# Spreading the router's logits over four steps of TensorE, and moving one weight subtraction from VectorE to GpSimd

## The chip, the cores and the metric

The kernel runs on one core of one Trainium2 chip. The metric is the device time of one execution in microseconds, lower is better. The engines are named as in the profile: PE is TensorE (PEld its weight loads), DVE is VectorE, ACT is ScalarE, POOL is GpSimd, and SP is the queue that issues most of the DMAs.

## The reference, cut to what matters

Eight sequences of 512 tokens with 256 features go through four residual layers: attention, a mixture of eight SwiGLU experts with the best two taken, a Mamba block, and a second mixture of eight experts. Every layer is fed the layer norm of x.

```python
x = L0_attn_x                                   # (8, 512, 256)
x = x + _L0_attn_ref(_layernorm(x), ...)        # 16 heads of 16, rotary, softmax, out projection
x = x + _L0_ffn_ref(_layernorm(x), ...)         # 8 experts, top 2, F = 352
x = x + _L1_attn_ref(_layernorm(x), ...)        # Mamba block, inner 512, state 16
x = x + _L1_ffn_ref(_layernorm(x), ...)         # 8 experts, top 2

# the router of the first expert layer, of which the change moves a part
logits = x @ router_weight                      # (4096, 256) @ (256, 8)
probs = softmax(logits, axis=-1)
_, topk_idx = top_k(probs, 2)
```

## The kernel before, in words

The four layers are phases, one behind the other. The change touches only the first, `attention_phase`, in which the attention runs, and beside it the routing of the tokens for the first expert layer, and the preparation of the first experts' weights.

The phase is a software pipeline written out by hand. The outer loop `for t in SLOTS` has a slot for each of 32 tiles (one is four heads of one sequence, `t` = 0 to 31) and some ahead and behind. In a slot TensorE has 16 steps, `for k in range(16)`. In each step it does one matmul of transposed scores for tile t (`scores_T`, line 983, into one of two banks `t_ps`) and one of plain scores for tile t + 2 (`scores`, line 992, into `s_ps`). ScalarE takes the exponent of each transposed score (`exp`, line 550). VectorE takes row maxima of the plain scores, eight in a slot, one for two steps (`max_pair`, line 706). TensorE may run two steps ahead of `exp`, and its `scores` of maximum m waits for `max_pair` m - 2; the last maximum of a slot is number 8u + 8. Steps 2, 6, 10 and 14 have the product with the values besides (`values`, line 1003), step 3 the transpose of the maxima (line 1009), step 8 the query and key product for a later sequence (`queries_keys`, line 1019), step 12 the value projection.

The routing goes sequence by sequence (`batch(t, lag)` says which, every fourth slot). Four slots carry it on: lag 10 transposes normalised rows, lag 11 makes the logits, lag 12 and 13 choose the experts and count places. The logits of one sequence are four token tiles (`logits(n, a, bank)`, a = 0 to 3, line 1059), with two products each in full fp32, eight columns wide, into the one bank `f_ps`, which is shared with steps 8 and 12, with the transpose of the maxima and others. `take_bank` keeps them apart: it waits for whatever must have emptied the bank, and its argument is what the next user has to wait for. `r_z` says that VectorE has taken the logits out (`differences`, lines 774 and 775, between the third and the fourth `max_pair` of its slot); they wait for `r_logits`, which comes with token tile a = 3. The lag 11 slots in this loop are t = 11, 15, 19, 23 and 27. The logits of the last three sequences are made in slots 30 and 31 and behind, with code of their own.

The weights of expert k of the next layer are loaded while attention still runs, and split into an upper part in fp32r and a remainder: ScalarE makes the upper part (`upper_piece`, line 115), another engine subtracts (`lower_parts`, line 129, two operations of 128x1088). For expert 0 ScalarE does it in slot 27, and VectorE subtracts in its tail, between `take_rows(n - 1, 1, ...)` and `differences(n - 1, ...)`, while TensorE is in slot 30. Expert 1 follows later in the same tail. The next phase's TensorE waits for `lo_done` ahead of its first tile.

POOL in a slot: Newton steps for a normalisation (`newton`, lines 282 to 288, if there is a sequence for it, as in slot 29), the split of the maxima (lines 481 and 483), the split of queries and keys, `merge_heads` (lines 458, 460, 463), then layer norm, the bias (line 429) and the scatter of rows (line 443). Its loop for slot 28 ends with `merge_heads(27)`.

## Time and profile before

| | |
|---|---|
| median of 3 runs | 2119.03 us (2118.62 to 2119.91) |
| the profiled execution | 2119.03 us |
| its span, first to last instruction | 2117.2 us |
| mean granted TensorE clock | 0.943 of full |
| busy | PE 1884.2, DVE 1654.2, ACT 1280.1, POOL 1427.7 us |

Busy shares are means over phases with different limits, so they say little about one phase. What lies around the span is the difference of 1.8 us to the execution's own time. The granted clock is given as a share of full speed: 1.00 is 2.4 GHz and 0.50 is 1.2 GHz. Line numbers are those of the kernel before.

### The profile page before, as it was taken

The numbers are of one execution on the slowest core, as the hardware profiler recorded it, in microseconds if no ns is written. First come the engines' busy times: TensorE is split into PE (matmuls) and PEld (weight loads), VectorE is DVE, ScalarE is ACT, GpSimd is POOL, SyncE is SP. The second block draws the span as 40 slices with busy tenths as digits, with TensorE's granted clock in tenths as the row PEclk, the third lists the DMA queues.
The fourth block names the chain that finished last, engine by engine and source line by source line (L and its number), as shares of the span: only waits on it lengthen the run. The fifth ranks groups of instructions, "written<-read, shape, count | busy, mean of one in ns | idle before, by whom it ended". The sixth has DMA issues, their size and how long they took to land.

```text
span 2117.2 us, 32322 instructions
## 1 busy us (share of the span) xinstructions
PE 1884.2 (89%) x9878; PEld 1104.5 (52%) x9878; DVE 1654.2 (78%) x2242; ACT 1280.1 (60%) x2736; POOL 1427.7 (67%) x1238
## 2 busy tenths in 40 slices
PE   3699999999974999966899999999999999779998
PEld 2344444444444999963445454535353544247776
DVE  4588888888855656530899999999999999976664
ACT  3177766677753433326787878777777766734443
POOL 4344545543352444430999999999999999966665
PEclk8599999999976999987999999999999999999999
DMA  5766665555254544640313030405040405200100
GB/s 106 120 103 115 104 104 117 121 122 117 61 178 127 105 74 77 139 104 28 152 50 131 33 148 10 171 1 179 0 180 0 171 0 182 89 30 29 37 27 29
DMA packets 231395, 194.35 MB, mean 92 GB/s; under 512 B 147219, under 2 KB 200235, under 8 KB 230716
## 3 DMA queue, kind: packets, MB, share of 16 engines
q1 hardware_dynamic: 205498, 163.33, 29.1%
q0 software_dynamic: 13296, 17.77, 5.0%
q10 hardware_dynamic: 12434, 11.18, 1.9%
q8 instruction: 85, 1.39, 0.3%
q14 instruction: 82, 0.67, 0.1%
HBM read 138.15 MB, written 54.08 MB: 91 GB/s over the span
## 4 chain that ended last, share of the span: by engine, by line
POOL 34%; PE 12%; issue 7%; ACT 1%; DVE 1%; DMA 0%; POOLq 0%; DVEq 0%; ACTq 0%
POOL mb_dbu L2191 22%; POOL mb_hp L2197 10%; PE mb_da_ps L2003 9%; POOL mb_dtu L2203 1%; PE mb_f_ps L2433 1%; PE mb_f_ps L1964 1%; PE mb_f_ps L2437 0%; PE mb_f_ps L2451 0%; PE mb_y_ps L1982 0%; PE mb_f_ps L1953 0%; PE mb_f_ps L2441 0%; DVE mb_da_ps L2373 0%; DVE mb_hp L2371 0%; ACT mb_res L2267 0%; ACT mb_xin L2270 0%
## 5 line engine op out<-in xcount | busy, mean ns | idle before, releaser
L2191 POOL TENSOR_TENSOR mb_dbu<-mb_dtu,mb_bbc 128x1024 f32<-128x1024 f32 x256 | 599.2, 2366 | 5.2 <-DVE mb_da_ps L2373 2.4
L550 ACT ACTIVATE ex_plain<-at_t_ps 128x512 f32<-128x512 f32 x512 | 289.7, 596 | 170.8 <-PE at_t_ps L983 169.6
L2373 DVE TENSOR_TENSOR_SCAN mb_da_ps<-mb_da_ps,mb_dbu 128x1024 f32<-128x1024 f32 x160 | 365.3, 2283 | 4.6 <-ACT mb_da_ps L2245 3.3
L2414 PE MATMUL mb_y_ps<-mb_hc,lw_ident 128*128 128x512 f32 x640 | 314.6, 615 | 38.6 <-DVE mb_hc L2380 37.9
L706 DVE TENSOR_REDUCE at_mx<-at_s_ps 128x2 f32<-128x1024 f32 x256 | 310.7, 1218 | 33.2 <-PE at_s_ps L992 31.2
L992 PE MATMUL at_s_ps<-ex_w 48*128 48x512 f32 x512 | 226.1, 499 | 16.1 <-DVE at_mx L706 16.1
L983 PE MATMUL at_t_ps<-ex_w 64*128 64x512 f32 x512 | 219.8, 483 | 12.2 <-ACT ex_plain L550 6.9
L2197 POOL TENSOR_TENSOR mb_hp<-mb_hp,mb_cbc 128x1024 f32<-128x1024 f32 x96 | 226.7, 2361 | 0.0
L2371 DVE TENSOR_TENSOR_SCAN mb_hp<-mb_da_ps,mb_dbu 128x1024 f32<-128x1024 f32 x96 | 218.9, 2280 | 8.5 <-POOL mb_dbu L2191 7.4
L1390 POOL DMA_INDIRECT x<-m_o,m_xs x71 | 113.7, 1601 | 163.3 <-DMA x<-m_o,m_xs 85.1
L2414 PEld LDWEIGHTS mb_y_ps<-mb_hc,lw_ident 128*128 128x128 f32 x640 | 118.9, 193 | 198.3 <-issue 127.7
L2380 DVE TENSOR_TENSOR mb_hc<-mb_da_ps,mb_cbc 128x1024 f32<-128x1024 f32 x160 | 195.4, 1221 | 12.5
L2414 PE MATMUL mb_y_ps<-mb_hp,lw_ident 128*128 128x512 f32 x384 | 185.5, 606 | 14.5 <-POOL mb_hp L2197 14.5
L983 PEld LDWEIGHTS at_t_ps<-ex_w 64*128 64x128 f32 x512 | 85.7, 191 | 177.4 <-ACT ex_plain L550 148.0
L2244 ACT ACTIVATE mb_da_ps<-mb_dt,lw_a_neg 128x512 f32<-128x512 f32 x256 | 172.6, 674 | 0.0
L2245 ACT ACTIVATE mb_da_ps<-mb_dt,lw_a_neg 128x511 f32<-128x511 f32 x256 | 171.9, 671 | 0.0
L2243 ACT ACTIVATE mb_da_ps<-mb_zero 128x1 f32<-128x1 f32 x256 | 43.0, 168 | 203.3 <-DVE mb_hc L2380 162.8
L1495 PE MATMUL m_y_ps<-ex_w,m_xsT_hi 128*128 x568 | 157.2, 338 | 0.0
L1003 PE MATMUL at_o_ps<-ex_plain 128*32 128x512 f32 x1024 | 143.6, 634 | 0.8 <-ACT ex_plain L550 0.7
L1645 POOL TENSOR_TENSOR m_odd<-m_odd,m_odd_in 128x256 f32<-128x256 f32 x96 | 70.8, 737 | 94.0 <-ACT m_odd_in L1765 89.4
L2414 PEld LDWEIGHTS mb_y_ps<-mb_hp,lw_ident 128*128 128x128 f32 x384 | 73.9, 195 | 105.2 <-issue 78.0
L1901 DVE SCALAR_TENSOR_TENSOR m_x<-mb_da_ps,m_small,m_x 128x256 f32<-128x256 f32 x128 | 61.8, 483 | 79.5 <-PE mb_da_ps L2003 76.8
(355 smaller groups left out, 4097.9 us busy)
## 6 DMA issues: line engine op xcount, KB each, us to landing
mb_bbc<-mb_scr SPq DMA_DIRECT2D x64, 512.0 KB, 5.9
mb_cbc<-mb_scr SPq DMA_DIRECT2D x64, 512.0 KB, 6.4
ex_w<-at_scr SPq DMA_DIRECT2D x126, 128.0 KB, 3.8
m_xs<-rt_rows SPq DMA_DIRECT2D x71, 129.0 KB, 2.2
at_scr<-at_qk_hi SPq DMA_DIRECT2D x32, 256.0 KB
ex_w<-at_scr SPq DMA_DIRECT2D x126, 64.0 KB, 3.8
at_scr<-at_qk_lo SPq DMA_DIRECT2D x28, 256.0 KB
at_xin<-in_x SPq DMA_DIRECT2D x32, 128.0 KB, 3.9
```

The source lines that it names most:

```text
L550: act.activation(probs[:, c, h, :], t_ps[:, k % 2, :], ACT.Exp, scale=SCALE).then_inc(exp_done, 1)
L706: dve.tensor_reduce(out, s_ps[:, m % 2, :, :], AX.X, ALU.max).then_inc(max_done, 1)
L983: pe.matmul(t_ps[:, k % 2, :], of_head(kst, r, h, 64, c), of_head(qst, r, h, 64), start=True, stop=True).then_inc(t_ready, 1)
L992: last = pe.matmul(s_ps[:, m % 2, a, :], of_head(qst, u % 4, h + 2 * a, 48, c), of_head(kst, u % 4, h + 2 * a, 48), start=True, stop=True)
L2003: last = pe.matmul(L.o_ps[:, u % 4, :], rows, w[:, e, kt, :], start=(m == 0), stop=(m == 5))
L2191: pool.tensor_tensor(dbu[:, q % 3, :, :], dtu_2, bbc[:, 2 * p:2 * p + 2, :], ALU.mult).then_inc(S["dbu_ready"], 1)
L2197: pool.tensor_tensor(hp[:, r, :, :], hp[:, r, :, :], cbc[:, 2 * p:2 * p + 2, :], ALU.mult).then_inc(S["hp_ready"], 1)
L2244: act.activation(da_ps[:, q % 2, 0, :], dt[:, d % 2, :], ACT.Exp, scale=a_neg[:, d, 2 * p:2 * p + 1])
L2371: dve.tensor_tensor_scan(hp[:, t % 3, :, :].rearrange("p j t -> p (j t)"), da, add, 0.0, ALU.mult, ALU.add).then_inc(S["scan_done"], 1)
L2373: dve.tensor_tensor_scan(da, da, add, 0.0, ALU.mult, ALU.add).then_inc(S["scan_done"], 1)
L2380: dve.tensor_tensor(hc[:, t % 2, :, :], da_ps[:, r, :, :], cbc[:, 2 * p:2 * p + 2, :], ALU.mult).then_inc(S["hc_ready"], 1)
L2414: last = pe.matmul(y_ps[:, v % 2, :], ident[:, :], src[:, j, :], start=False, stop=(q == tile_last[v] and j == 1))
```

## The change

Two edits. The logits of a sequence are made one token tile in each of the steps 4, 5, 6 and 7, where there were two in step 4 and two in step 5; the wait for `r_z` is set behind the last of them. And `lower_parts` of expert 0 is called by POOL at the end of its slot 28, no longer by VectorE in its tail.

```diff
@@ attention_phase, gpsimd @@
                     if (n := batch(t, 13 + c)) is not None:
                         pool.wait_ge(v_ps_ready, min(t + 3, NT))
                         scatter(n, c)
+                if t == 28:
+                    experts.lower_parts(pool, 0)
                 if t == NT - 1:
                     scatter(NB - 3, 0)
@@ attention_phase, vector @@
             take_rows(n - 1, 1, score_bank(3))
-            experts.lower_parts(dve, 0)
             differences(n - 1, score_bank(0))
@@ attention_phase, tensor @@
-                    if k in (4, 5) and (n := batch(t, 11)) is not None and t < NT - 2:
-                        f_free = take_bank([(R["r_z"], n + 1)] if k == 5 else [])
-                        logits(n, 2 * (k - 4), f_ps)
-                        logits(n, 2 * (k - 4) + 1, f_ps)
+                    if 4 <= k < 8 and (n := batch(t, 11)) is not None and t < NT - 2:
+                        f_free = take_bank([(R["r_z"], n + 1)] if k == 7 else [])
+                        logits(n, k - 4, f_ps)
```

## Rows read from the trace of the kernel before

**Rows 1.** The page, part 4: the chain that ended last, by engine

```profile
POOL 34%; PE 12%; issue 7%; ACT 1%; DVE 1%; DMA 0%; POOLq 0%; DVEq 0%; ACTq 0%
```

**Rows 2.** Waits, 110 to 600 us: who waited for whom, us, times, longest

```profile
ACT ex_plain L550 <- PE at_t_ps L983: 145.2, 187, 2.1
...
DVE at_mx L706 <- PE at_s_ps L992: 28.9, 61, 2.0
```

**Rows 3.** Slots 8, the five with logits (first, last, sum), and 28

```profile
core 0: us, PE busy (x) PEld busy (x) DVE busy (x) ACT busy (x) POOL busy (x), PEclk, DMA share, GB/s
220.06:235.15 15.09, 14.77 (x143) 6.64 (x142) 13.06 (x20) 10.86 (x24) 8.52 (x20) 1.00 0.67 107
...
266.95:287.97 21.02, 19.96 (x160) 9.68 (x158) 15.22 (x27) 10.84 (x23) 8.21 (x13) 0.84 0.61 112
...
535.32:552.87 17.55, 17.10 (x152) 8.11 (x150) 12.72 (x21) 12.27 (x25) 4.61 (x5) 0.81 0.29 72
sum 94.82, PE 91.67 PEld 45.00 DVE 70.85 ACT 55.26 POOL 41.38; mean PE 18.33 PEld 9.00 DVE 14.17 ACT 11.05 POOL 8.28
...
552.87:567.03 14.16, 13.53 (x136) 5.63 (x134) 13.75 (x24) 11.42 (x24) 5.01 (x11) 1.00 0.26 63
```

**Rows 4.** Stretch ahead of the first fall; first two of five falls; their sum

```profile
266.70:270.10 3.40, 3.21 (x23) 2.27 (x21) 2.85 (x5) 2.33 (x5) 0.72 (x2) 1.00 1.14 282
270.10:276.90 6.80, 6.80 (x22) 3.01 (x22) 2.84 (x8) 2.20 (x4) 0.00 (x0) 0.50 0.43 69
341.80:345.20 3.40, 3.40 (x13) 2.18 (x10) 1.43 (x3) 1.60 (x3) 0.28 (x1) 0.50 0.51 128
...
sum 23.60, PE 23.34 PEld 10.10 DVE 10.64 ACT 10.53 POOL 2.88; mean PE 4.67 PEld 2.02 DVE 2.13 ACT 2.10 POOL 0.57
```

**Rows 5.** Timeline of slot 11, PE and DVE: start, us, engine, line, idle before

```profile
267.84 1.06 PE L1059 MATMUL at_f_ps<-at_rw,at_wraw 128*128 128x8 f32 x8 [0.18 <-ACT at_nm L601]
...
269.26 1.14 PE L1059 MATMUL at_f_ps<-at_rw,at_wraw 128*128 128x8 f32 x8
...
269.39 1.23 DVE L706 TENSOR_REDUCE at_mx<-at_s_ps 128x2 f32<-128x1024 f32 x1 [0.43 <-PE at_s_ps L992]
...
270.54 0.18 DVE L774 TENSOR_REDUCE at_zmax<-at_f_ps 128x4 f32<-128x32 f32 x1
...
273.78 1.23 DVE L706 TENSOR_REDUCE at_mx<-at_s_ps 128x2 f32<-128x1024 f32 x1 [2.03 <-PE at_s_ps L992]
...
277.03 0.75 DVE L866 TENSOR_SCALAR at_qk<-at_f_ps,at_bqk 128x512 f32<-128x512 f32 x1 [2.03 <-PE at_f_ps L1019]
```

**Rows 6.** Timeline of VectorE's tail and TensorE's slot 30

```profile
588.89 3.56 DVE L129 TENSOR_TENSOR ex_w<-ex_plain,ex_w 128x1088 fp32r<-128x1088 f32 x2
...
591.39 1.06 PE L1059 MATMUL at_s_ps<-at_rw,at_wraw 128*128 128x8 f32 x8
...
592.48 0.19 DVE L774 TENSOR_REDUCE at_zmax<-at_s_ps 128x4 f32<-128x32 f32 x1
```

**Rows 7.** Timeline, POOL and DVE side by side; L782 over all (ns min/median/max)

```profile
282.39 2.36 POOL L429 TENSOR_TENSOR ex_plain<-ex_plain 128x1024 f32<-128x1024 f32 x1
...
283.36 1.45 DVE L782 TENSOR_TENSOR at_pr<-at_pr,at_scale 128x32 f32<-128x32 f32 x1
...
623.32 1.53 POOL L463 TENSOR_TENSOR ex_plain<-ex_plain,at_rsum 128x512 f32<-128x512 f32 x1
...
623.55 1.35 DVE L726 TENSOR_TENSOR at_masks<-at_ties,at_rank 128x32 f32<-128x32 f32 x1
...
L782 DVE TENSOR_TENSOR at_pr<-at_pr,at_scale x8: 191/306/1445, 283.4 to 645.9; 128x32 f32<-128x32 f32 x8
```

**Rows 8.** Timeline around the end of slot 28: POOL, DVE and PE

```profile
560.51 1.54 POOL L463 TENSOR_TENSOR ex_plain<-ex_plain,at_rsum 128x512 f32<-128x512 f32 x1
...
563.33 0.19 DVE L720 TENSOR_TENSOR at_ties<-at_left,at_pay 128x32 f32<-128x32 f32 x1
...
563.85 1.23 DVE L706 TENSOR_REDUCE at_mx<-at_s_ps 128x2 f32<-128x1024 f32 x1
...
565.27 0.40 PE L983 MATMUL at_t_ps<-ex_w 64*128 64x512 f32 x1
```

## The prediction, made before the result was known

> **What bounds the kernel now.** I read the page first, its chain that ended last: 34% of the span is POOL, from lines of the Mamba phase [rows 1]. Both edits lie far ahead of that, in the attention phase, roughly the first third of the span. The later phases start when it is done, so what it gains or loses at its own end reaches the end of the kernel in full; the question is what sets its pace. The waits show that no engine does alone: ScalarE waited 145 us for transposed scores of TensorE, and VectorE 29 us for its plain scores [rows 2]. TensorE, VectorE and ScalarE run in a ring, two steps apart, and over a whole slot TensorE and VectorE are both nearly full. Time by slot shows it: slot 8, with no routing product, took 15.09 us with TensorE busy for 14.77 and VectorE for 13.06. The five slots that hold the router's logits (t = 11, 15, 19, 23, 27) took 21.02 us in the first and 17.55 in the last, 94.82 us together, and slot 28 took 14.16 us with VectorE busy for 13.75 of them [rows 3].
>
> Then I asked why the logits slots are so long, by short stretches. Each has a fall of the granted clock to 1.2 GHz, half of 2.4: five falls, 23.6 us together, in which TensorE was busy for 23.34. Ahead of the first it had been busy for 3.21 of 3.40 us at full clock, so that it was not idle before it fell; but it streamed only eight columns per matmul in the logits [rows 4]. The first logits products and those of the next step take 1.06 and 1.14 us, with one pair of score matmuls between them, and the fall begins as they end [rows 5].
>
> **The change part by part.**
> *Logits spread over four steps (k = 4 to 7) in place of two.* The same eight matmuls a slot (16 records), nothing added: about 0.53 us for one token tile (half of 1.06), 2.1 us for four [rows 5]. Spread out, steps 4 to 7 each hold one score pair and 0.53 us of logits, and the attention product of step 6 now stands in the middle of the logits, not behind them. If that keeps the clock up, the gain is at most half of the falls, as the engine was busy all through: 23.6 / 2 = 11.8 us.
> Against it stands VectorE's order. It takes the logits between its third and fourth maximum of the slot (L774 between two L706). The third began at 269.39 in slot 11 and took 1.23 us; logits were ready then, and L774 began at 270.54 with no wait [rows 5]. Worked through at full clock from 267.84: logits end at 268.4, pair of step 5 at 268.8, logits 269.3, pair of step 6, attention product to 270.7, logits 271.2, pair of step 7, last logits 272.2. The third maximum is done at 270.2, so VectorE now waits 2.1 us, with the fourth maximum, ready at 271.7, queued behind. The two small operations are done at 272.75. TensorE is released for the query and key product of step 8 (it uses the same bank) about 0.25 us later than it gets there, and step 10's scores, which need the fourth maximum, about 0.1 us late: 0.35 us a slot for TensorE. VectorE then ends its fourth maximum at 274.8 in place of 275.0 (273.78 + 1.23), takes the query chunk right behind it at 274.8, where it took it at 277.03 [rows 5]. So of the 3.4 us that the fall of 6.8 us cost, 2.2 come back and 1.2 stay with VectorE's new wait. I take the same 1.2 off in each of the five: 11.8 - 6.0 = 5.8 us gained if no fall is left. If all five are left, nothing comes back and TensorE's 0.35 us is paid five times: 1.7 us lost. The rows don't show which it will be: the products are half as thick, but the thin stretch is longer, 4.4 us (267.84 to 272.2) in place of 2.5 (to 270.4), with an attention product in it. I take the middle: (5.8 - 1.7) / 2 = 2.0 us gained.
>
> *The subtraction for expert 0 off VectorE's tail.* Two subtractions of 128x1088 ran there from 588.89 for 3.56 us. Right behind them L774 began at 592.48; but the logits it reads are TensorE's, from 591.39 for 1.06 us, up to 592.45 [rows 6]. What is late next is therefore already there: VectorE would have waited to 592.45 anyhow, and the gain is 0.03 us, taken as nothing. It can't be more unless those logits come sooner, and they are as they were.
>
> *The same subtraction on POOL at the end of slot 28.* It waits for ScalarE's upper pieces of slot 27, long made. POOL's merge of heads ends at 562.05 (560.51 + 1.54); the two operations follow at once. Price: the trace has POOL at 2.36 us for 128x1024, so 2.36 x 1088 / 1024 = 2.51 us each, 5.0 us, up to 567.1 [rows 7, 8]. Queued behind on POOL are the seven small Newton steps, whose result ScalarE wants in step 4 of slot 29, and the split of the maxima, whose rows TensorE wants a slot later; both would be late by a microsecond or two at most, and ScalarE stands in that time anyway, by what follows.
> What is not hidden is VectorE. Where POOL reads SBUF in a tensor operation, a VectorE operation with two SBUF inputs stands still: L782, a 128x32 product begun at 283.36, took 1.45 us and ended at 284.81, with POOL's 128x1024 addition from 282.39 to 284.75; its shortest is 0.19. Two in a row are each held by a POOL operation of their own: L726, at 623.55, stood to 624.90 for the POOL operation that began at 623.32, before it [rows 7]. In slot 28 VectorE begins such an operation at 563.33 (L720), the next one behind it, and then the last maximum at 563.85 [rows 8]. The first is held to POOL's end at 564.6; POOL's second operation then takes its turn and holds L721 to 567.1. The last maximum begins at 567.2: 3.4 us late. TensorE needs it for its scores in step 2 of slot 29, to which it came at 565.27, and stands for 3.2 us, ScalarE behind it. VectorE has next to no slack to make it good (0.4 us in slot 28 [rows 3]). So +3.4 us; the bounds are 0 (POOL elsewhere when these two come) and 3.4.
> The Trainium skill, SBUF — State Buffer, "Who interferes with whom", has the pair of ports shared as an exclusive lock for the whole instruction, for two-input VectorE operations against GpSimd reads, and no conflict for a reduction. By this rule the sum is the same 3.4; were the hold only a sharing of bandwidth, it would be about 0.4 us. The row, which ends with POOL's operation, agrees.
> The stand of 3.2 us may also bring a fall of TensorE's clock in slot 29. The falls after the logits were 3.4 or 6.8 us; one of 3.4 costs 0 (VectorE sets the pace) to 1.7 us. I take 0.5.
>
> Sum: -2.0 + 0 + 3.4 + 0.5 = +1.9 us on the profiled execution's own 2119.03, which is also the median of the three runs: 2120.9 us.
>
> **The rivals.**
> *All falls go, and POOL's hold is paid.* -5.8 + 3.4 + 0.5 = -1.9: 2117.1 us. For it: each fall follows the two thick clumps of logits. Against it: the thin stretch gets longer.
> *Falls go and the hold misses.* If VectorE reaches its two small operations in slot 28 before 562, or after 567, there is no hold: -2.0 to -5.8, about 2114.5 us. It speaks for it that slot 27's falls end differently and may shift the two engines against each other; against it, that 5 us of POOL must miss a pair of operations in a slot where VectorE never idles.
> *Slower: the falls stay and the hold is paid with a fall behind it.* +1.7 + 3.4 + 1.7 = +6.8: 2125.8 us. Its place is the last maximum of slot 28, and it decides once at most one of the five falls goes (from +0.2% = 4.2 us on).
> The Trainium skill, TensorE: Matmul & The Clock Gate, "Why this matters for your kernels", puts drops down to idle gaps between bursts. By it the spread would leave the clock as it is and the hold in slot 28 would bring a fall, which is the slower case. The rows disagree in part, as the clock fell after stretches in which the engine was busy throughout.
>
> **How the numbers follow.** A difference of 0.2%, 4.2 us, is about what a measurement here can tell from none. Chances: the likeliest case (hold paid, about half of the falls gone, 2117.5 to 2123.2) 0.48; all falls gone with the hold 0.14; hold missed 0.14, of which 0.10 reaches beyond 0.2%; slower 0.24. So faster 0.12 (the 0.10 and a tail of the second case), same 0.65, slower 0.23. The range goes from the sum of the best bounds (-5.8 with a little over the hold's zero, 2114) to near the worst (2126).
>
> **What would show it.** In the changed kernel: L1059 in groups of four records, one a step; a wait of about 2 us of VectorE for L1059 ahead of L774 in the five slots; the granted clock in those slots, five falls or fewer; on POOL two operations of L129 of 2.5 us near 560; L720 and L721 behind them at over 1 us each, then a wait of TensorE's L992 for L706 of about 3 us, and slot 28 to 29 longer than 14.16 us by as much; L774 in the tail waiting for L1059 at about its old distance. The prediction is wrong if the five slots shorten by over 8 us, if L721 stays at 0.19 us, or if the tail's L774 moves forward by more than the rest.

## The result, and the profile after

The changed kernel is slower: a median of 2136.55 us (2134.21 to 2138.44, 4 runs) against 2119.47 us of the kernel before in the same series (2118.62 to 2122.36, 4 runs). The ratio is 1.0078, with a 95% interval of 1.006 to 1.0095, or 17.1 us by the medians. The forecast was 2120.9 us within 2114 to 2126: no change was the likeliest case, and the time lies outside the range on the side of the slower rival, beyond it too. The profiled execution took 2136.86 us, its span is 2135.1 us, and the mean granted clock 0.939. One operation of `lower_parts` stands on line 129 in both kernels; most lines of the attention phase are one or two further on (L706 is now L708, L720 and L721 are L722 and L723, L774 is L776, L983 is L984, L992 is L993, L1003 is L1004, L1059 is L1060).

The page's chain that ended last is word for word the line of [rows 1]: the later phases are as they were, and what the attention phase loses reaches the end.

The waits of 110 to 600 us (who waited for whom, us, times, longest). Against [rows 2] ScalarE waits 9 us more for transposed scores, and VectorE has a wait for the logits that is new:

```profile
ACT ex_plain L552 <- PE at_t_ps L984: 153.8, 186, 3.7
...
DVE at_zmax L776 <- PE at_f_ps L1060: 16.6, 5, 4.1
```

Time by slot, from one transpose of the maxima to the next, as in [rows 3]: slot 8, then the logits slots 11, 15, 19, 23 and 27, then 28 and 29.

```profile
218.98:234.07 15.09, 14.78 (x144) 6.65 (x142) 13.08 (x20) 10.87 (x24) 8.52 (x20) 1.00 0.66 102
265.87:288.35 22.48, 21.62 (x159) 10.66 (x158) 15.20 (x27) 11.06 (x23) 8.26 (x13) 0.77 0.58 110
337.56:360.04 22.48, 21.63 (x159) 10.67 (x157) 15.26 (x27) 11.06 (x23) 11.63 (x18) 0.77 0.59 132
409.15:430.68 21.53, 21.34 (x160) 10.67 (x158) 13.85 (x25) 10.79 (x21) 9.29 (x11) 0.76 0.49 114
479.61:496.84 17.23, 16.87 (x157) 8.60 (x155) 13.69 (x23) 10.89 (x21) 7.68 (x8) 1.00 0.64 146
540.84:558.73 17.89, 16.51 (x151) 7.77 (x150) 12.59 (x21) 12.49 (x25) 4.58 (x5) 0.90 0.30 68
558.73:576.04 17.31, 14.05 (x136) 5.72 (x134) 16.97 (x25) 11.43 (x24) 9.90 (x13) 1.00 0.24 52
576.04:594.98 18.94, 18.41 (x136) 7.77 (x134) 12.09 (x22) 12.46 (x24) 6.16 (x8) 0.64 0.07 24
```

Slot 8 is the same to 0.01 us. The five logits slots take 101.61 us in place of 94.82. Their share of half clock can be read from the column PEclk: at 0.77 a slot of 22.48 us has 2 x 0.23 x 22.48, about 10.3 us, at 1.2 GHz. Slots 11, 15 and 19 have a fall of 10.2 us each, slot 23 has none and is the one that got shorter, and slot 27 has one of 3.4. That last one is of another kind: it begins 8.0 us into the slot, behind 3.4 us in which TensorE was busy for only 2.20. Slot 28 goes from 14.16 to 17.31 us at full clock, so by a stand and not by the clock, and slot 29 from 14.46 to 18.94 us at 0.64.

That makes an account of the 17.8 us by which the two spans differ: -1.1 before slot 11 starts, +6.8 in the five logits slots, +0.15 in the slots between, +3.15 in slot 28, +4.5 in slot 29, and +4.3 from slot 30 to the end. The last of these goes with the clock too. These are the 110 us from the start of slot 30, before and after:

```profile
581.49:691.49 110.00, 68.86 (x318) 46.67 (x318) 61.84 (x170) 49.16 (x94) 45.17 (x46) 0.67 0.47 148
594.98:704.98 110.00, 69.96 (x302) 45.07 (x302) 55.53 (x163) 46.84 (x89) 42.06 (x44) 0.63 0.47 148
```

By the same reading that is about 73 us at 1.2 GHz before and 81 after. The first matmul of line 1495, in the next phase, starts 89.2 us after slot 30 before and 91.9 after, so that 2.7 of the 4.3 us are already there.

The first fall of 10.2 us in three pieces, with the 3.4 us ahead of it, to be read against [rows 4]:

```profile
265.50:268.90 3.40, 3.21 (x23) 1.97 (x25) 3.29 (x6) 2.42 (x6) 0.72 (x2) 1.00 1.10 279
268.90:272.30 3.40, 3.40 (x15) 1.41 (x8) 0.20 (x1) 0.60 (x2) 0.00 (x0) 0.50 0.91 136
272.30:275.70 3.40, 3.40 (x11) 2.55 (x12) 2.31 (x7) 1.62 (x3) 0.00 (x0) 0.50 0.02 7
275.70:279.10 3.40, 3.40 (x15) 0.98 (x13) 1.98 (x2) 1.64 (x4) 1.46 (x2) 0.50 0.02 5
```

TensorE was busy for 3.21 of 3.40 us ahead of it, as in the kernel before, and for all of each of the three pieces. The timeline of the same slot, PE and DVE, against [rows 5]:

```profile
266.77 0.61 PE L1060 MATMUL at_f_ps<-at_rw,at_wraw 128*128 128x8 f32 x4 [0.19 <-ACT at_nm L603]
...
267.73 0.61 PE L1060 MATMUL at_f_ps<-at_rw,at_wraw 128*128 128x8 f32 x4
...
268.70 1.79 PE L1004 MATMUL at_o_ps<-ex_plain 128*32 128x512 f32 x8
270.43 1.02 PE L1060 MATMUL at_f_ps<-at_rw,at_wraw 128*128 128x8 f32 x4
...
272.10 1.02 PE L1060 MATMUL at_f_ps<-at_rw,at_wraw 128*128 128x8 f32 x4
...
273.16 0.19 DVE L776 TENSOR_REDUCE at_zmax<-at_f_ps 128x4 f32<-128x32 f32 x1 [4.06 <-PE at_f_ps L1060]
```

The clock falls after the second group. The attention product and the last two groups run at half speed, 1.79 us for what takes 1.06 and 1.02 us for 0.61, and VectorE stands for 4.06 us where it stood for none.

The end of slot 28, POOL, DVE and PE, against [rows 8]:

```profile
567.87 4.95 POOL L129 TENSOR_TENSOR ex_w<-ex_plain,ex_w 128x1088 fp32r<-128x1088 f32 x2
...
569.20 1.23 DVE L722 TENSOR_TENSOR at_ties<-at_left,at_pay 128x32 f32<-128x32 f32 x1
...
570.47 2.40 DVE L723 TENSOR_TENSOR at_ties<-at_ties,at_order 128x32 f32<-128x32 f32 x1
...
572.90 1.23 DVE L708 TENSOR_REDUCE at_mx<-at_s_ps 128x2 f32<-128x1024 f32 x1
...
574.18 0.50 PE L993 MATMUL at_s_ps<-ex_w 48*128 48x512 f32 x1 [2.63 <-DVE at_mx L708]
```

This went as forecast, operation by operation: two subtractions of 4.95 us together, each of which holds one of VectorE's two operations to its own end (1.23 and 2.40 us in place of 0.19 each), the last maximum right behind, and TensorE's stand for it.

The tail, against [rows 6]:

```profile
604.87 1.06 PE L1060 MATMUL at_s_ps<-at_rw,at_wraw 128*128 128x8 f32 x8
605.96 0.19 DVE L776 TENSOR_REDUCE at_zmax<-at_s_ps 128x4 f32<-128x32 f32 x1 [3.50 <-PE at_s_ps L1060]
```

The subtraction of 3.56 us is gone and a wait of 3.50 us stands there. L776 comes 10.98 us after the start of slot 30 (594.98), before it was 10.99 (592.48 from 581.49).

### The profile page after: what moved, and what is told of

The parts are those of the page before. It is cut to its first block, busy times and chain, and to the rows that moved or that the text cites. A ratio compares the mean times of both kernels' runs of the same rounds, so it can differ in the third digit from the quotient of the medians.

```text
span 2135.1 us, 32322 instructions
## 1 busy us (share of the span) xinstructions
PE 1896.7 (89%) x9878; PEld 1108.9 (52%) x9878; DVE 1653.4 (77%) x2240; ACT 1282.4 (60%) x2736; POOL 1431.0 (67%) x1240
## 4 chain that ended last, share of the span: by engine, by line
POOL 34%; PE 12%; issue 7%; ACT 1%; DVE 1%; DMA 0%; POOLq 0%; DVEq 0%; ACTq 0%
POOL mb_dbu L2191 22%; POOL mb_hp L2197 10%; PE mb_da_ps L2003 9%; POOL mb_dtu L2203 1%; PE mb_f_ps L2433 1%; PE mb_f_ps L1964 1%; PE mb_f_ps L2451 0%; PE mb_y_ps L1982 0%; PE mb_f_ps L2437 0%; PE mb_f_ps L1953 0%; PE mb_f_ps L2441 0%; DVE mb_da_ps L2373 0%; DVE mb_hp L2371 0%; ACT mb_res L2267 0%; ACT mb_xin L2270 0%
## 5 line engine op out<-in xcount | busy, mean ns | idle before, releaser
L708 DVE TENSOR_REDUCE at_mx<-at_s_ps 128x2 f32<-128x1024 f32 x256 | 310.7, 1218 | 30.4 <-PE at_s_ps L993 28.5
L993 PE MATMUL at_s_ps<-ex_w 48*128 48x512 f32 x512 | 228.8, 504 | 19.0 <-DVE at_mx L708 17.4
L984 PE MATMUL at_t_ps<-ex_w 64*128 64x512 f32 x512 | 224.1, 493 | 11.0 <-ACT ex_plain L552 5.8
L984 PEld LDWEIGHTS at_t_ps<-ex_w 64*128 64x128 f32 x512 | 87.5, 195 | 175.3 <-ACT ex_plain L552 141.9
L1004 PE MATMUL at_o_ps<-ex_plain 128*32 128x512 f32 x1024 | 148.7, 655 | 0.8 <-ACT ex_plain L552 0.7
```

Of the source, the lines that this page charges most:

```text
L708: dve.tensor_reduce(out, s_ps[:, m % 2, :, :], AX.X, ALU.max).then_inc(max_done, 1)
L984: pe.matmul(t_ps[:, k % 2, :], of_head(kst, r, h, 64, c), of_head(qst, r, h, 64), start=True, stop=True).then_inc(t_ready, 1)
L993: last = pe.matmul(s_ps[:, m % 2, a, :], of_head(qst, u % 4, h + 2 * a, 48, c), of_head(kst, u % 4, h + 2 * a, 48), start=True, stop=True)
```

## The experiments

All were timed beside the kernel before, in three series, in which its median was 2120.75 us (2113.54 to 2125.43, 27 runs), 2119.95 us (2113.03 to 2126.1, 35 runs) and 2118.75 us (2113.38 to 2125.4, 23 runs). The first two series ran on one chip. The third ran on another: the whole change with the hold taken out, half of the hold, the changed kernel once more, and the two pairs far apart. The ratios are the ones to go by: single executions of one kernel differ by up to 13 us here. A fall that is given a length below was read off the granted clock of that run's trace.

### The parts of the change

**The spread alone.**

```diff
-                    if k in (4, 5) and (n := batch(t, 11)) is not None and t < NT - 2:
-                        f_free = take_bank([(R["r_z"], n + 1)] if k == 5 else [])
-                        logits(n, 2 * (k - 4), f_ps)
-                        logits(n, 2 * (k - 4) + 1, f_ps)
+                    if 4 <= k < 8 and (n := batch(t, 11)) is not None and t < NT - 2:
+                        f_free = take_bank([(R["r_z"], n + 1)] if k == 7 else [])
+                        logits(n, k - 4, f_ps)
```

> The logits are spread over steps 4 to 7, and the subtraction stays in VectorE's tail. Theory 1 (the spread itself lengthens the clock falls: three falls of 10.2 us in slots 11, 15 and 19 of the changed kernel, where they were 6.8, 3.4 and 3.4): the start of slot 28 comes 6.9 us later than before, as in the changed kernel, and the total is about 2126 us, 7 above before. Rival 2 (the spread costs nothing lasting, the whole 17 us comes from POOL's operations): 2119 plus or minus 1 us. Rival 3 (the spread gains by itself, as I worked it out, and only together with the other edit is it lost): 2113 to 2117 us.

Measured: 2129.46 us median (2113.54 to 2132.45, 11 runs), ratio 1.0032 (1.0014 to 1.0051), or about 6.8 us slower. Its slots 11, 15 and 19, and the sum of the five:

```profile
268.29:286.94 18.65, 17.53 (x159) 8.90 (x158) 15.18 (x27) 11.12 (x23) 8.22 (x13) 1.00 0.69 127
336.15:358.56 22.41, 21.55 (x159) 10.77 (x157) 15.25 (x27) 11.05 (x23) 11.68 (x18) 0.77 0.58 130
407.64:429.44 21.80, 21.58 (x160) 10.71 (x158) 14.21 (x25) 10.77 (x21) 9.30 (x11) 0.77 0.51 115
...
sum 99.32, PE 95.40 PEld 47.72 DVE 70.92 ACT 56.31 POOL 41.45; mean PE 19.08 PEld 9.54 DVE 14.18 ACT 11.26 POOL 8.29
```

The same instructions give two kinds of slot. Slot 11 has no fall and takes 18.65 us, 2.4 less than before; slots 15 and 19 have one of 10.2 us each and take 2.9 and 3.3 more. So the spread is a gamble: its fastest run, 2113.54 us, equals the fastest of the kernel before in that series, and in most executions it loses. Slot 28 starts at 558.78 us, 5.9 later than before, as in the changed kernel (558.73); the 6.9 of the expectation was a slip.

**The second edit alone.**

```diff
+                if t == 28:
+                    experts.lower_parts(pool, 0)
...
-            experts.lower_parts(dve, 0)
```

> POOL does the subtraction of expert 0 at the end of slot 28; the logits stay two and two. Theory 1 (VectorE's two-input operations are held to the end of POOL's, TensorE then stands for about 3 us, and a clock fall follows it): slot 28 is 3.2 us longer, slot 29 some 4 us, L721 takes over 2 us, total about 2129 us, 10 above before. Rival 2 (the hold alone, no fall): 2122.5 us. Rival 3 (it costs nothing without the spread, since VectorE and POOL meet differently): 2119 us.

Measured: 2126.44 us (2124.44 to 2134.03, 10 runs), ratio 1.0037 (1.0023 to 1.005). Its slots 28 and 29:

```profile
552.24:569.74 17.50, 14.22 (x136) 5.71 (x134) 17.12 (x26) 11.45 (x24) 9.93 (x13) 0.99 0.23 52
569.74:586.36 16.62, 15.62 (x135) 6.43 (x133) 11.94 (x21) 12.36 (x24) 5.95 (x8) 0.81 0.08 27
```

Slot 28 has 3.3 us more by the hold, and slot 29, in which nothing was changed, 2.2 more with a fall of 6.8 us behind TensorE's stand (some 4 were expected).

**The subtraction on GpSimd in slot 30.** The same work off VectorE, but not where it holds anything.

```diff
+                if t == NT - 2:
+                    experts.lower_parts(pool, 0)
                 if (u := tile(t - 1)) is not None:
                     merge_heads(u)
...
-            experts.lower_parts(dve, 0)
```

> As the last one, but POOL does the same two operations in slot 30, ahead of its merge of heads 29, where VectorE has no operation with two SBUF inputs. If the price of slot 28 is the hold of VectorE and not POOL's own time: same as before, 2118 to 2120 us, no VectorE operation longer than before, and L774 in the tail still waits for TensorE's logits (gain of taking the subtraction off VectorE: nothing). Rival (any 5 us of POOL late in attention delays the chain, or the subtraction in VectorE's tail was on the path): 2122 us or more, or below 2116 us.

Measured: 2119.12 us (2113.88 to 2125.59, 11 runs), ratio 0.9996 (0.9981 to 1.0012). In the timeline GpSimd works from 584.77, and VectorE's tail waits as in the changed kernel:

```profile
584.77 4.95 POOL L129 TENSOR_TENSOR ex_w<-ex_plain,ex_w 128x1088 fp32r<-128x1088 f32 x2
...
594.08 0.19 DVE L776 TENSOR_REDUCE at_zmax<-at_s_ps 128x4 f32<-128x32 f32 x1 [3.50 <-PE at_s_ps L1060]
```

So 5 us of GpSimd's time cost nothing there, and 3.56 us less of VectorE's tail gain nothing.

**The whole change with the hold taken out:** the spread, and the subtraction in slot 30, both as above.

> The whole change, but GpSimd subtracts in its slot 30 and not at the end of slot 28, where VectorE begins two operations with two SBUF inputs. Theory 1 (the second edit costs only by its place): as the spread alone, 2125 to 2130 us, with slot 28 at 14.2 us, L721 at 0.19 us and no fall behind it in slot 29. Rival (the two edits hurt each other through the shared bank and the tail): 2133 us or more.

Measured: 2126.66 us (2116.61 to 2130.97, 12 runs), ratio 1.0033 (1.0019 to 1.0048), the ratio of the spread alone. Slots 28 and 29 took 14.18 and 14.45 us at full clock. With this and the last run, the second edit costs by its place alone.

**Half of the hold.** Of the two subtractions the first on GpSimd in slot 28, the second in VectorE's tail, behind a wait for the first.

```diff
+    def lower_half(self, eng, k, i):
+        eng.wait_ge(self.hi_done, k + 1)
+        if i:
+            eng.wait_ge(self.half_done, 1)
+        hi, lo, raw = self.piece(k, i, 2)
+        eng.tensor_tensor(lo, raw, hi, ALU.subtract).then_inc(self.lo_done if i else self.half_done, 1)
...
+                if t == 28:
+                    experts.lower_half(pool, 0, 0)
...
-            experts.lower_parts(dve, 0)
+            experts.lower_half(dve, 0, 1)
```

> The second edit alone and half of it: the first of the two subtractions on GpSimd at the end of slot 28, the second stays in VectorE's tail. Two of them in slot 28 gave 5.7 us more, 3.3 of it in slot 28 and 2.1 in slot 29 by a fall of 6.8 us behind TensorE's stand. Theory 1 (each GpSimd subtraction holds one of VectorE's two operations to its own end): L720 held to about 564.7, L721 at 0.19 us, the last maximum some 0.9 us late, no fall in slot 29: 2120 to 2122.5 us. Rival (the cost is not by the hold but by GpSimd's lateness for its Newton steps and the split of the maxima): half of 5.7, about 2123 to 2124 us, with L721 short in both.

Measured: 2119.98 us (2115.96 to 2122.83, 12 runs), ratio 1.0001 (0.999 to 1.0012). The timeline (here L730 and L731 are the two operations), and slots 28 and 29:

```profile
559.42 2.51 POOL L130 TENSOR_TENSOR ex_w<-ex_plain,ex_w 128x1088 fp32r<-128x1088 f32 x1
...
560.76 1.23 DVE L730 TENSOR_TENSOR at_ties<-at_left,at_pay 128x32 f32<-128x32 f32 x1
562.02 0.19 DVE L731 TENSOR_TENSOR at_ties<-at_ties,at_order 128x32 f32<-128x32 f32 x1
```

```profile
550.27:565.38 15.11, 14.07 (x136) 5.74 (x134) 14.77 (x25) 11.44 (x24) 7.53 (x12) 1.00 0.25 59
565.38:579.82 14.44, 13.22 (x135) 5.53 (x133) 11.86 (x22) 12.14 (x24) 5.95 (x8) 1.00 0.09 31
```

One subtraction holds one operation. Slot 28 is 0.95 us longer, and behind this shorter stand the clock does not fall. The price is not in proportion: one subtraction costs 0.95 us, two cost 3.3 in slot 28 and a fall as well. The rival was that GpSimd's lateness for its Newton steps costs the time. They began 11.75 us after the start of slot 28 here, where they began 10.19 before and 14.17 in the changed kernel. So this run rules out that 1.6 us of lateness cost anything: slot 29 took 14.44 us. For the 4.0 us of the changed kernel its own trace answers: in its slot 29 ScalarE's waits are all for TensorE, none for GpSimd.

**The changed kernel once more,** word for word.

> The changed kernel once more, word for word, for a second profile of it beside the others. Its two parts alone gave 2129.5 (spread) and 2126.4 us (subtraction on GpSimd in slot 28) against 2120.75, 8.7 and 5.7 us. Theory 1: the parts add up, 2133 to 2137 us, and the logits slots show falls of 10.2 us or none at all, never of 3.4 us; slot 28 is 17.3 us long again. Rival: the first profile was a poor draw, and the kernel is nearer to 2128 us.

Measured: 2137.91 us (2129.56 to 2142.56, 5 runs), ratio 1.0081 (1.006 to 1.0103). Its profile is of the fastest of these executions, and shows slots 11, 15 and 19, the sum of the five, and slots 28 and 29 thus:

```profile
268.03:289.44 21.41, 20.36 (x159) 10.50 (x157) 15.20 (x27) 10.96 (x23) 8.23 (x13) 0.84 0.61 113
338.66:357.31 18.65, 17.53 (x160) 8.89 (x158) 15.24 (x27) 11.11 (x23) 11.64 (x18) 1.00 0.72 154
406.39:423.96 17.57, 17.20 (x159) 8.86 (x158) 13.74 (x25) 10.89 (x21) 9.31 (x11) 1.00 0.58 132
...
sum 93.99, PE 89.70 PEld 45.72 DVE 70.46 ACT 56.31 POOL 41.46; mean PE 17.94 PEld 9.14 DVE 14.09 ACT 11.26 POOL 8.29
...
553.16:571.96 18.80, 15.53 (x135) 5.96 (x133) 17.37 (x26) 11.44 (x24) 9.95 (x13) 0.91 0.21 48
571.96:590.83 18.87, 18.34 (x135) 7.77 (x134) 11.86 (x20) 12.48 (x24) 6.16 (x8) 0.64 0.07 24
```

The same kernel, other falls: slots 15 and 19 have none and take 3.8 and 4.0 us less than in its first profile. My theory that a spread slot has a fall of 10.2 us or none was too neat: slots 11 and 27 have one of 6.8 each. Slots 28 and 29 are the other way: 9.0 us more than in the kernel before, with one fall of 17.1 us that begins in slot 28, which took 18.80 us and not 17.3.

### What the falls come from

**One token tile a slot.** In the five slots only token tile 3 is computed; the logits of tiles 0 to 2 of those sequences are left out.

```diff
-                    if k in (4, 5) and (n := batch(t, 11)) is not None and t < NT - 2:
-                        f_free = take_bank([(R["r_z"], n + 1)] if k == 5 else [])
-                        logits(n, 2 * (k - 4), f_ps)
-                        logits(n, 2 * (k - 4) + 1, f_ps)
+                    if k == 5 and (n := batch(t, 11)) is not None and t < NT - 2:
+                        f_free = take_bank([(R["r_z"], n + 1)])
+                        logits(n, 3, f_ps)
```

> Leaves work out: in the slots 11, 15, 19, 23 and 27 only the logits of token tile 3 are made (step 5), so that the router of the first five sequences reads what else lies in the bank. It prices the logits and their falls together. Theory 1 (the falls come from TensorE's thin products): hardly a fall is left in the five slots, each 15.5 to 16.5 us, 94.8 us down to about 80, total about 2105 us. Rival (the falls come from something else in those slots, such as the wait for the maxima in step 3): five falls stay, and the total is at most 8 us (5 x 1.6) below before, 2111 us.

Measured: 2104.33 us (2101.27 to 2106.62, 4 runs), ratio 0.9925 (0.9904 to 0.9946). The five slots:

```profile
266.70:283.17 16.47, 15.57 (x148) 7.08 (x146) 15.01 (x27) 10.67 (x23) 8.22 (x13) 1.00 0.74 132
...
sum 77.39, PE 74.78 PEld 34.02 DVE 69.67 ACT 54.43 POOL 41.48; mean PE 14.96 PEld 6.80 DVE 13.93 ACT 10.89 POOL 8.30
```

None has a fall, and they take 17.4 us less. The products that were left out are worth 5 x 3 x 0.53 = 8.0 us at full clock, so more than half of it is the clock (and VectorE's waits). In these slots it is the thin products that bring the falls. They are not the only thing that does: slot 26, which has no logits, has a fall of 3.4 us in this run and in the kernel before. There TensorE was less busy ahead of it; before:

```profile
522.40:525.80 3.40, 2.42 (x14) 1.01 (x16) 3.31 (x7) 2.77 (x6) 0.00 (x0) 1.00 0.25 45
```

**The spread with VectorE's take moved.** Of the possible reasons for the long falls, VectorE's new wait was the one to take away first. The logits are spread as in the change, the subtraction stays in the tail, and VectorE takes the logits behind its fourth maximum.

```diff
-                if (n := batch(t, 11)) is not None:
-                    differences(n, f_ps)
...
                 max_pair(ahead, 3)
+                if (n := batch(t, 11)) is not None:
+                    differences(n, f_ps)
```

> Logits spread over steps 4 to 7 as in the change, with nothing on GpSimd, and VectorE takes them behind its fourth maximum and no longer ahead of it. The spread alone gave 2129.5 us, with clock falls of 10.2 us in two of the five logits slots of its profile and none in two others. Theory 1: the falls are so long because the thin products now lie over four steps; VectorE's order is not their cause: falls of 0 or 10.2 us again, 2127 to 2131 us. Theory 2: VectorE's wait for the last logits, with the fourth maximum queued behind it, starves TensorE at half clock and keeps the fall alive: without that wait the falls are 3.4 or 6.8 us as in the kernel before, 2117 to 2122 us. In both TensorE may stand some 0.5 us a slot ahead of the query and key product of step 8, since its bank now comes free behind the fourth maximum.

Measured: 2125.81 us (2113.62 to 2130.66, 12 runs), ratio 1.0023 (1.0007 to 1.0039). VectorE doesn't wait for logits any more in slot 11, and the five slots sum to about what they did:

```profile
277.37 0.18 DVE L774 TENSOR_REDUCE at_zmax<-at_f_ps 128x4 f32<-128x32 f32 x1
```

```profile
269.70:292.17 22.47, 21.63 (x159) 10.71 (x158) 15.20 (x27) 11.06 (x23) 8.27 (x13) 0.77 0.59 108
...
sum 100.21, PE 96.50 PEld 48.05 DVE 71.01 ACT 56.04 POOL 41.26; mean PE 19.30 PEld 9.61 DVE 14.20 ACT 11.21 POOL 8.25
```

Falls of 10.2 us in slots 11, 15 and 19 again, so the wait is not their cause. The median is lower than that of the spread alone and 1.2 us below the range of the first theory, but the two intervals overlap: whether the moved take gains a little is open.

**All four token tiles in step 5.** The other way round: thicker and shorter.

```diff
-                    if k in (4, 5) and (n := batch(t, 11)) is not None and t < NT - 2:
-                        f_free = take_bank([(R["r_z"], n + 1)] if k == 5 else [])
-                        logits(n, 2 * (k - 4), f_ps)
-                        logits(n, 2 * (k - 4) + 1, f_ps)
+                    if k == 5 and (n := batch(t, 11)) is not None and t < NT - 2:
+                        f_free = take_bank([(R["r_z"], n + 1)])
+                        for a in range(4):
+                            logits(n, a, f_ps)
```

> All four token tiles of logits in step 5, eight matmuls (16 records) in one stretch of 2.1 us, no others moved. Theory 1 (what counts is over how long a stretch the thin products lie): the falls get shorter or rarer than in the kernel before, 0 or 3.4 us in place of 3.4 and 6.8: 2110 to 2117 us. Rival (what counts is how thick they lie): falls of 6.8 us or more in all five slots, 2122 us or above. Either way TensorE's bank and VectorE's take of the logits stand as in the kernel before.

Measured: 2116.84 us (2114.47 to 2120.11, 12 runs), ratio 0.999 (0.9977 to 1.0002). The falls are of 3.4 us in slots 11, 15 and 19 and of 6.8 in 23 and 27; the five slots sum to 93.73 us. The time fits the first theory (2110 to 2117), the ratio can't tell it from no change, and all five falls are there, as the rival had it. Thick and short is at any rate better than thin and long.

**Two groups with the query and key product between them.** One token tile in each of the steps 4, 5, 9 and 10. VectorE takes two tiles where it took four, and the other two behind its fifth maximum (the lines that call it there are left out below); `r_half` and `r_zh` are new semaphores for the first half.

```diff
+            def half_differences(n, h):
+                z_in = f_ps[:, 2 * h * E0:(2 * h + 2) * E0].rearrange("p (k e) -> p k e", k=2)
+                dve.wait_ge(R["r_logits"] if h else R["r_half"], n + 1)
+                steps(dve.tensor_reduce(zmax[:, 2 * h:2 * h + 2], z_in, AX.X, ALU.max))
+                zb = zmax[:, 2 * h:2 * h + 2].unsqueeze(2).broadcast_to([P, 2, E0])
+                dve.tensor_tensor(pr[:, 2 * h:2 * h + 2, :], z_in, zb, ALU.subtract).then_inc(R["r_z"] if h else R["r_zh"], 1)
...
-                    if k in (4, 5) and (n := batch(t, 11)) is not None and t < NT - 2:
...
+                    if k in (4, 5, 9, 10) and (n := batch(t, 11)) is not None and t < NT - 2:
+                        a = (4, 5, 9, 10).index(k)
+                        f_free = take_bank([(R["r_zh"], n + 1)] if a == 1 else [(R["r_z"], n + 1)] if a == 3 else [])
+                        logits(n, a, f_ps)
```

> The four token tiles in two groups with the query and key product between them: one tile each in steps 4, 5, 9 and 10, VectorE takes the first two where it took all four, and the other two behind its fifth maximum; ScalarE's exponent of the logits goes from step 10 to step 11. Theory 1 (falls come where thin products lie close together, and not otherwise; with a single tile a slot there was no fall and the five slots took 77.4 us together): no falls, 77.4 + 5 x 3 x 0.53 = 85.4 us for the five slots in place of 94.8, so 9.4 less on 2120.75: about 2111 us. Rival (the number of thin products in a slot decides, wherever they stand): falls as before or as in the spread, 2120 to 2130 us. A wait of some 0.5 us of TensorE ahead of step 9's logits, for VectorE's take of the query chunk, may come on top, five times: 2 us.

Measured: 2114.72 us (2111.82 to 2118.82, 12 runs), ratio 0.9978 (0.9968 to 0.9987). The five slots sum to 89.29 us, with falls of 3.4 us in slots 11 and 15 and none in the others: neither theory in full, and faster than the kernel before by its interval.

**The second group in step 10 alone.** As the last one, but tiles 2 and 3 back to back in step 10.

```diff
+                    if k in (4, 5) and (n := batch(t, 11)) is not None and t < NT - 2:
+                        f_free = take_bank([(R["r_zh"], n + 1)] if k == 5 else [])
+                        logits(n, k - 4, f_ps)
+                    if k == 10 and (n := batch(t, 11)) is not None and t < NT - 2:
+                        f_free = take_bank([(R["r_z"], n + 1)])
+                        logits(n, 2, f_ps)
+                        logits(n, 3, f_ps)
```

> As the split version, but the last two token tiles stand together in step 10, behind the product with the values, where the bank is long free. Theory 1: no falls, about 2111 us, without the wait in step 9. If two tiles back to back (1.06 us) are enough for a fall by themselves, one is seen that begins in step 10 or 11, and the time is between this and 2120.75 us. Rival (the number of thin products in a slot decides): 2120 to 2130 us.

Measured: 2116.37 us (2113.3 to 2122.34, 12 runs), ratio 0.9988 (0.9978 to 0.9999). The five slots sum to 88.31 us, with falls of 3.4 us in slots 11, 15 and 19. They begin 2.5 to 2.8 us into the slot, so ahead of step 10: it is the first group that brings them, and the second, back to back, brings none.

**Two pairs, far apart.** Tiles 0 and 1 back to back in step 5, tiles 2 and 3 in step 10 as in the last one.

```diff
+                    if k == 5 and (n := batch(t, 11)) is not None and t < NT - 2:
+                        f_free = take_bank([(R["r_zh"], n + 1)])
+                        logits(n, 0, f_ps)
+                        logits(n, 1, f_ps)
```

> The logits in two pairs, two token tiles back to back in step 5 and two in step 10, with the query and key product between them. One tile each in steps 4, 5, 9 and 10 gave 2114.7 us, two falls of 3.4 in four slots; steps 4, 5 and a pair in 10 gave 2116.4 us with three; all four in step 5 2116.8 us with three of 3.4 and two of 6.8. Theory 1 (closeness counts, two pairs far apart are short enough): at most two falls of 3.4 us, 2112 to 2116 us. Rival (a pair is as bad as four): 2117 us or more, with falls in all five slots.

Measured: 2112.2 us (2109.09 to 2114.13, 6 runs), ratio 0.9957 (0.9942 to 0.9972): the fastest that does the whole work, by 9 us against the kernel before. Slot 23, and the sum of the five:

```profile
469.28:484.98 15.70, 15.65 (x157) 8.16 (x155) 13.60 (x24) 10.57 (x21) 7.62 (x8) 1.00 0.66 146
...
sum 87.19, PE 84.99 PEld 42.02 DVE 72.11 ACT 54.92 POOL 41.43; mean PE 17.00 PEld 8.40 DVE 14.42 ACT 10.98 POOL 8.29
```

Three falls of 3.4 us, in slots 11, 15 and 19, where at most two were expected, and none in 23 and 27. Its interval lies below that of the version with steps 4, 5 and a pair in 10, and just overlaps that of the single tiles; both of those were timed in another series, on the other chip.

How many falls one profile shows doesn't tell these versions apart. The run with half of the hold, in which the logits stand as before, has none in slots 23 and 27 either. It allows a comparison without the clock, though. Its slot 23:

```profile
472.66:489.35 16.69, 16.39 (x158) 8.23 (x156) 13.81 (x23) 10.65 (x21) 7.68 (x8) 1.00 0.63 148
```

With the two pairs the slot takes 15.70 us, also at full clock: 1.0 us less with the same products. Slot 27 took 15.06 against 15.47, both without a fall, and slots 15 and 19 took 19.10 and 18.25 against 19.51 and 18.53 in the kernel before, with a fall of 3.4 us in each of the four. So by these profiles some 2 us of the 9 are the order of the work and not the clock.

## Why the prediction was wrong

Point by point, by its own steps.

*The spread: this is the step that failed.* The prediction said "I take the middle: (5.8 - 1.7) / 2 = 2.0 us gained". It measured 6.8 us lost (3 to 11 by the interval). The mistake is in the bounds under it: "If all five are left, nothing comes back" let a fall that stays be as long as it was, 3.4 or 6.8 us, so that the worst was TensorE's 0.35 us five times. The falls that stayed were mostly longer: 10.2 us in two to three of the five slots in four of the five profiles with spread logits. Over the five slots together these profiles have 34.0, 27.2, 30.6, 37.4 and 13.6 us at half clock, and the four in which the logits stand as before 23.8, 27.2, 27.2 and 13.6. The slots themselves sum to 94.0 to 102.7 us, mean 99.6, against 91.4 to 96.6, mean 94.8. So two single profiles could have shown it either way, and it is the ratios that show the loss. The text named the reason, a thin stretch of 4.4 us in place of 2.5, and used it only against the gain, never for a loss. The 0.35 us itself held: with a fall of 6.8 us in both, slot 11 took 21.41 us spread (the changed kernel's second profile) and 21.02 before, 0.39 more. The upper bound was right in kind: where no fall came, slots 15 and 19 took 18.65 and 17.57 us against 19.51 and 18.53 of before, though these had only 3.4 us at half clock each. Put together from the slots without a fall of the different spread profiles (18.65, 18.65, 17.57, 17.23 and 15.59 us), the five would take 87.7 us, 7.1 less than before, where 5.8 were forecast. The half of its length that a fall was taken to cost at most has a clean pair now, slot 15 of the changed kernel: 22.48 us with a fall of 10.2 and 18.65 with none, 3.8 us where half would be 5.1.

*VectorE's new wait.* Forecast as 2.1 us at full clock in each of the five slots, and 2.23 us in slot 23, the one without a fall. In the five together it was 16.6 us, 3.3 on average, and 4.06 in slot 11, where the fall began between the groups. It was there, and it was not the cause of the falls, as the version with the take moved shows.

*The subtraction off the tail.* Forecast as nothing, and nothing it was: 10.98 us into slot 30 in place of 10.99, and a ratio of 0.9996 where it was done alone in a harmless place.

*GpSimd's hold in slot 28.* Forecast 3.4 us; measured 3.15 in the changed kernel and 3.3 in the second edit alone. The order (first operation to the end of the first subtraction, second to the end of the second) was right, and TensorE's stand was near, 2.63 us where 3.2 were forecast. The Trainium skill, SBUF — State Buffer, "Who interferes with whom", has this as an exclusive lock for the whole instruction, and the traces agree: 1.23 and 2.40 us for operations of 0.19, each ending with GpSimd's. The rows show besides that two VectorE operations in a row are held by two of GpSimd's in a row, one each.

*The fall behind the stand.* Taken as 0.5 us, at most 1.7, from falls of 3.4 us. This term was mis-sized: the falls were 6.8, 13.6 and 17.1 us long in the three profiles with both subtractions in slot 28, and slot 29 took 2.2, 4.5 and 4.4 us more (with 1.3 more in slot 28 in the last). A stretch of the trace shows how idle TensorE was ahead of the fall: busy for 1.92 of 3.40 us in the changed kernel, where it was busy for all of them at this place before. The first line is of the kernel before, the other two of the changed one.

```profile
563.69:567.09 3.40, 3.40 (x23) 1.47 (x19) 3.19 (x7) 2.17 (x4) 0.99 (x5) 1.00 0.00 0
572.70:576.10 3.40, 1.92 (x12) 0.59 (x12) 3.30 (x7) 0.00 (x0) 1.58 (x8) 1.00 0.00 0
576.10:589.70 13.60, 13.16 (x107) 5.97 (x107) 8.54 (x17) 8.65 (x17) 2.20 (x4) 0.50 0.01 4
```

In the other two profiles it was busy for 1.60 and 0.90 of the 3.40 us. The trace of the kernel before had a warning that the bound left out, since it was taken from the logits slots alone: from 601.20 to 631.90 us, in the tail, TensorE ran at half clock for 30.7 us in one piece, busy for 23.06 of them.

The Trainium skill, TensorE: Matmul & The Clock Gate, "Why this matters for your kernels", puts drops in the middle of a kernel down to idle gaps between bursts of matmuls; the fall in slot 29 is of that kind, though its stand, 2.63 us, is a little shorter than the gap that the row names. Those in the five logits slots of the kernel before are not, as TensorE was busy for 3.21 to 3.40 of the 3.40 us ahead of each, and the version with one token tile a slot has none. There the measurement decides.

*The sum.* 6.8 us for the spread and 7.8 for the second edit (0.37% of 2120.75) make 14.6, and the whole change measured 0.78% and 0.81%, 16.5 to 17.2. Within the intervals the parts add up. The slower rival had the right mechanisms (hold and fall behind it, nothing gained by the spread) and stopped at 2125.8 us because it let no fall be longer than those in the logits slots of the one profile of before. The rival with the hold missed has a slip in its sum that changed nothing: -2.0 to -5.8 on 2119.03 is 2113.2 to 2117.0, so its middle is 2115.1, and its lower end lies below the range's 2114.

*What stays open.* Why a fall over spread logits mostly lasts 10.2 us and one over dense ones 3.4 or 6.8 was not isolated. What is shown is the order of the times over the spacings, and that VectorE's order is not the reason. Nor is it known what sets the length of the fall behind the stand: 1.60, 1.92 and 0.90 of 3.40 us busy were followed by 6.8, 13.6 and 17.1. The 4.3 us from slot 30 on look like a draw of the clock and not an effect: the same kernel took 1536.9 us for that stretch in its second profile, with a mean clock of 0.67 over the 110 us from slot 30 as in the kernel before, and the twelve experiments took 1534.9 to 1540.2.

## What to carry to other kernels

Where a bound is taken from the length of the falls in one profile, it is not a bound: a change that makes a thin stretch longer, or adds a stand, can make a fall longer than those that the profile shows in that place, so that the worst case needs a term of its own. In this kernel small matmuls that stream few columns were better kept in short groups with dense work between the groups (ratio 0.9957) than thinned out over four neighbouring steps (1.0032); that is worth trying elsewhere, and part of the gain was not the clock's. And work that is moved to GpSimd costs nothing or several microseconds by what VectorE does beside it, as slots 30 and 28 show: look for its operations with two SBUF inputs, count how many stand in a row, and put the work where there are none.

## What the runs showed of the hardware that was not expected

The clock fell with TensorE busy. Over a stretch of 3.4 us with 3.21 busy, in which the last products stream eight columns each, it went from 2.4 to 1.2 GHz, and with a quarter of these products it did not fall in any of the five slots.

Where and for how long it falls is not a property of the kernel alone. The changed kernel, word for word the same, had in slots 15 and 19 falls of 10.2 us in one execution and none in another, 3.8 and 4.0 us apart; the kernel before, whose instructions didn't change either, ranged from 2113.0 to 2126.1 us over 35 runs. One profile of such a kernel is one draw, and a difference of a few microseconds in a slot should be looked for in a second profile before it is believed.
